# The slices' matmuls spread in four parts between the experts' layers

## The reference, cut to what matters

```
x = x + L0_gnn(layernorm(x), ...)        # first graph stage
x = x + L0_ffn(layernorm(x))             # top-2 experts
# second graph stage: attention over the edges
x_proj = (layernorm(x) @ W)
e_exp  = exp(alpha_src[row] + alpha_dst[col] - max over the edges of col)
out    = segment_sum(e_exp * x_proj[row], col) / segment_sum(e_exp, col)
x = x + out
# second expert stage: 8 dense experts of three layers on every node
feat = mean(layernorm(x)); w = softmax(feat @ Wr + br)
h = relu(bn(x_n @ W1 + b1)); h = relu(bn(h @ W2 + b2)); y = h @ Wo + bo
x = x + sum_e w_e * y_e
```

## Time and profile before

| | |
|---|---|
| runs (3), median | 5944.67 us |
| profiled execution, device time | 5958.87 us |
| its span | 5956.8 us |
| PE, share of the span | 4136.2 us, 69% |
| POOL, share of the span | 3178.3 us, 53% |
| DVE, ACT | 28%, 18% |
| granted TensorE clock, mean | 0.791 |

### The profile page before, as it was taken

How to read it: one execution, slowest core, us unless ns; L and a number is a source line. 1 busy time by engine, 2 the same in 40 slices (tenths; PEclk the granted TensorE clock), 3 DMA queues, 4 the chain that set the end, 5 groups by cost and what they waited for, 6 DMA issues and landing times. The chain is left out here.

```text
span 5956.8 us, 65813 instructions
## 1 busy us (share of the span) xinstructions
PE 4136.2 (69%) x20734; PEld 3330.2 (56%) x20734; DVE 1657.3 (28%) x5503; ACT 1082.2 (18%) x2144; POOL 3178.3 (53%) x3331
## 2 busy tenths in 40 slices
PE   1666666666666666666997267777777777777778
PEld 1665565656665656566886145554555455455546
DVE  5232322323222323233566011111121111112112
ACT  2010110101010101011564011121122112122212
POOL 5555555555555555553222665655555565556551
PEclk7777777777777777777998577877887787788779
DMA  5222222222222222221112433333333333333331
GB/s 170 73 83 84 83 83 85 80 86 80 85 81 83 82 83 83 83 82 54 59 48 68 133 94 99 96 93 98 96 98 91 98 97 94 96 96 100 92 97 42
DMA packets 223401, 522.56 MB, mean 88 GB/s; under 512 B 59660, under 2 KB 93918, under 8 KB 223332
## 3 DMA queue, kind: packets, MB, share of 16 engines
q0 software_dynamic: 155392, 430.52, 26.1%
q1 hardware_dynamic: 35768, 44.79, 2.4%
q10 hardware_dynamic: 32172, 46.39, 2.3%
HBM read 475.24 MB, written 46.24 MB: 88 GB/s over the span
## 5 line engine op out<-in xcount | busy, mean ns | idle before, releaser
L695 POOL DMA_INDIRECT ring<-xn,index x1588 | 1501.9, 946 | 1165.9 <-ACT index L708 693.1
L1697 POOL DMA_INDIRECT ring<-table,index x1616 | 1543.3, 955 | 1071.5 <-ACT index L1712 606.3
L814 PE MATMUL bank<-spare,ring 128*128 128x160 f32 x6448 | 1059.2, 328 | 265.4 <-issue 182.2
L814 PEld LDWEIGHTS bank<-spare,ring 128*128 128x128 f32 x6448 | 1022.9, 215 | 289.2 <-issue 217.7
L1892 PE MATMUL bank<-ring,acc 128*32 128x264 f32 x3232 | 577.6, 544 | 470.2 <-issue 415.0
L1766 ACT ACTIVATE ework<-bank,bn 128x256 f32<-128x256 f32 x800 | 406.5, 560 | 1506.2 <-remote 998.1
L824 PE MATMUL bank<-cells,wblk 128*128 128x128 f32 x1632 | 396.7, 365 | 399.2 <-issue 392.5
L1892 PEld LDWEIGHTS bank<-ring,acc 128*32 128x32 f32 x3232 | 187.5, 137 | 798.6 <-issue 774.0
L824 PEld LDWEIGHTS bank<-cells,wblk 128*128 128x128 f32 x1632 | 320.5, 262 | 467.5 <-issue 464.9
L1913 PE MATMUL bank<-acc,wa 128*128 (+1 forms) x1600 | 500.0, 463 | 90.9 <-ACT acc L1757 65.5
L824 PE MATMUL bank<-spare,wblk 128*128 128x128 f32 x1600 | 340.0, 355 | 286.9 <-issue 284.4
(11 more groups left out here) (272 smaller groups left out, 3019.9 us busy)
## 6 DMA issues: line engine op xcount, KB each, us to landing
ring<-table,index POOLq DMA_INDIRECT x1616
ring<-xn,index POOLq DMA_INDIRECT x1612
sums<-acc ACTq DMA_DIRECT2D x101, 132.0 KB
acc<-sums ACTq DMA_DIRECT2D x25, 264.0 KB
table<-frow SPq DMA_DIRECT2D x24, 264.0 KB, 3.0
nx<-in_x ACTq DMA_DIRECT2D x24, 256.0 KB
x<-nx ACTq DMA_DIRECT2D x24, 256.0 KB
fx<-x SPq DMA_DIRECT2D x24, 256.0 KB
```

What stands on the lines that cost most here:

```text
L695: pool.indirect_dma_start(ring[:, m * BT + t, :], None, k.xn_d, bass.IndirectOffsetOnAxis(ap=index[m][:, t:t + 1], axis=0)).then_inc(got[m ...
L814: ins = pe.matmul(win[q][:, h, :], ring[:, m * BT + q * QUAD + t, h * P:(h + 1) * P], onehot[:, (q * QUAD + t) % HELD, :], start=(t == 0), ...
L1697: pool.indirect_dma_start(ring[:, par * BT + t, :], None, k.table1_d, bass.IndirectOffsetOnAxis(ap=index[par][:, t:t + 1], axis=0)).then_i ...
```

## The change

PE no longer runs the 16 slice matmuls of batch b in one piece at the end of period b. It runs those of batch b-1 during period b in four parts of four matmuls: after layer 1 and layer 2 and layer 3 of sub-step 0, and after layer 1 of sub-step 1. The join of batch b-1 moves from sub-step 0 of period b to the end of that period. ACT's `keep_slices` and the staging of the next batch's offsets and index move from the period's start to behind layer 1's relu of sub-step 1; `move_window` and `keep_window` move to the period's end. DVE makes the next one-hots behind `gather_up` of sub-step 1 instead of that of sub-step 0.

```diff
@@ ACT, period
-                if window:
-                    keep_slices(b - 1)
-                if gathers and window:
-                    stage_near(b + 1, 1 - par)
-                    stage_index(b + 1, 1 - par)
...
                     for j2, e in experts(work_of, u, LAYER1):
                         relu(1, j2, e)
-                    if window and u == 0:
-                        move_window(b - 1, 1 - par)
-                        keep_window(b - 1, 1 - par)
+                    if window and u == 1:
+                        keep_slices(b - 1)
+                        if gathers:
+                            stage_near(b + 1, 1 - par)
+                            stage_index(b + 1, 1 - par)
...
                     for j2, e in experts(work_of, u, LAYER2):
                         relu(2, j2, e)
+                if window:
+                    move_window(b - 1, 1 - par)
+                    keep_window(b - 1, 1 - par)
@@ PE, slice_sums and period
-            def slice_sums(b, par, half, m, n):
-                pe.wait_ge(hots, b + 1)
...
-                for u in range(QUAD):
-                    for q in range(QUADS):
...
-                ins.then_inc(done, 1)
+            def slice_sums(b, par, half, u):
+                if u == 0:
+                    pe.wait_ge(hots, b + 1)
...
+                    for t in range(BT):
+                        wait_rows(pe, par, half, 0, 0, t)
+                for q in range(QUADS):
+                    t = q * QUAD + u
...
+                if u == QUAD - 1:
+                    ins.then_inc(done, 1)
...
+                last = (b - 1, 1 - par, half - 1 + par)
                 for u in range(2):
                     for j2, e in experts(work_of, u, LAYER1):
                         layer1(j2, e)
-                    if window and u == 0:
-                        join(b - 1, 1 - par)
+                    if window:
+                        slice_sums(*last, 3 * u)
                     for j2, e in experts(work_of, u, LAYER2):
                         layer2(j2, e)
+                    if window and u == 0:
+                        slice_sums(*last, 1)
                     for j2, e in experts(work_of, u, LAYER3):
                         layer3(j2, e)
+                    if window and u == 0:
+                        slice_sums(*last, 2)
+                    if window and u == 1:
+                        join(b - 1, 1 - par)
...
-                if gathers:
-                    slice_sums(b, par, half, m, n)
@@ DVE, period
-                if gathers:
-                    if not (isinstance(b, int) and b == 0):
-                        dve.wait_ge(windowed, b)
-                    one_hots(b + 1, 1 - par)
                 for j2, r in work_of:
                     if r == TURN + 2:
                         soft(j2)
                 for j2, e in experts(work_of, 1, GATHER):
                     gather_up(j2, e)
+                if gathers:
+                    if not (isinstance(b, int) and b == 0):
+                        dve.wait_ge(windowed, b)
+                    one_hots(b + 1, 1 - par)
                 for j2, r in work_of:
                     if r == TURN:
                         norm(j2)
```

More of the change, by code:

```diff
@@ L1881, in _ @@
             pe.wait_ge(p_load, 16 * 13)
-            def slice_sums(b, par, half, m, n):
-                pe.wait_ge(hots, b + 1)
-                if not (isinstance(b, int) and b == 0):
-                    pe.wait_ge(moved, b)
-                for t in range(BT):
-                    wait_rows(pe, par, half, m, n, t)
-                for u in range(QUAD):
-                    for q in range(QUADS):
-                        t = q * QUAD + u
-                        ins = pe.matmul(win[q * SLICE:(q + 1) * SLICE, :], onehot[:, par * BT + t, :],
-                                        ring[:, tile_at(par, m, t), :], start=(u == 0), stop=(u == QUAD - 1))
-                ins.then_inc(done, 1)
+            def slice_sums(b, par, half, u):
+                if u == 0:
+                    pe.wait_ge(hots, b + 1)
+                    if not (isinstance(b, int) and b == 0):
+                        pe.wait_ge(moved, b)
+                    for t in range(BT):
+                        wait_rows(pe, par, half, 0, 0, t)
+                for q in range(QUADS):
+                    t = q * QUAD + u
+                    ins = pe.matmul(win[q * SLICE:(q + 1) * SLICE, :], onehot[:, par * BT + t, :],
+                                    ring[:, tile_at(par, 0, t), :], start=(u == 0), stop=(u == QUAD - 1))
+                if u == QUAD - 1:
+                    ins.then_inc(done, 1)
             def join(b, par):
```

## The result

The changed kernel takes 6063.69 us (median of 4 runs, 6057.24 to 6070.47) against 5946.73 us for the kernel before (4 runs, 5944.37 to 5950.27): a ratio of 1.0198, 95% interval 1.0186 to 1.0210. It is 117 us slower; 148 us slower, 6093 us, was predicted. The profiled execution took 6070.47 us with a span of 6068.3.

The account below looks back on a forecast made before the run. PE was taken to be limited while a batch of gathers is under way. Transposition periods (24 x 5 = 120 us) and plain ones (28 us) summed to +148 us, giving 6093 us, own range 5985 to 6220.

Parts of the forecast that it names:

- the stall: PE's stretch of single MATMULs late in a batch's gathers, read as a limit beside gathers; 415.0 us idle before the slices.
- Term 1: PE's work ahead of done after the release, in periods without transposition: +0.4 us each, 28 us in all.
- upper bound: In plain periods, layer 1 and the last slice part follow the release at a low clock: 1.8 us more.
- lower bound: In plain periods, PE does all its work before the release: cycle 25.4 us, 0.6 us less.
- Term 2: Period with the transposition, where PE waits 8.4 us for one_hots and norm: +5 us, 24 times, 120 us.
- hand-made schedule: PE's pieces in the transposition's period timed from the first gather, G, to the next: 29.7 us, +3.7 us.
- the signal that I held to be late: The transposition's signal from PE to ACT, possibly 3 to 4 us late like the relu's: then +7 us.
- Term 3: Small costs: matmul shape switches, eight a period instead of two, hidden or 112 us; window's store, 0 to 3 us x 24.
- The stall goes: Rival: slices slow through themselves, so four early parts escape and the 415 us before them go; 5530 us, 7%.
- the clock stays down: Rival: PE's granted clock stays at 0.5 in free stretches, +4 us in every cycle; 6317 us, 8%.
- PE gets ahead: Rival: PE clears everything by the release in every period, each cycle 25.4 us; 5889 us, 10%.
- Only a rotation: Rival: terms 1 and 2 both near 0, no change; 5945 us, 5%.

Follow-up runs that it names:

- half_gathers: The kernel before with 8 of the 16 gathers of each merged-stage batch left out, slice matmuls reading the 8 gathered tiles twice: ratio 0.8337, 4967 us.
- tail_slices: The changed kernel with the fourth slice part right behind the third, and ACT's slice copy and casts ahead of layer 1's relu: ratio 1.0069 to the kernel before.
- norm_first: The changed kernel with DVE's norm put ahead of one_hots again: ratio 1.0168 to the kernel before.
- all_three: The changed kernel with norm ahead of one_hots, fourth slice part behind the third, index cast first, on chips without the stall: 0.9999, again 0.9996 to the kernel before.
- parted_done: The kernel before with done raised after each quarter of the slices, next gathers issued in quarters behind it, on chips without the stall: 0.9998, again 0.9998.
- norm_tail: The changed kernel with norm ahead of one_hots and the fourth slice part right behind the third: ratio 0.9982 to the kernel before.

## Why the prediction was right, and where it was not

The time, the sign and the mechanism came out: 6064 us measured for 6093, inside the own range of 5985 to 6220. The split of the sum did not: it was right as a sum because two terms were off in opposite directions, and that part of it is luck. Counted by the table, 44 us of the loss lie in the transposition's cycles, for which 120 were forecast, and 73 in the others, for which 28 were.

*What bounds.* The reading that the stall follows the gathers and not the slices held: half_gathers removed it (idle time before the slices 470.2 to 19.5 us), in the changed kernel it also sits on layer 1 and in tail_slices on layer 3. What the prediction could not know is that the program alone does not bring it about: three sets on other chips had none of it.

*Term 1, the tail of a plain period (+0.4 us taken, 28 us).* This is the step that failed most. Its upper bound had the tail as 14 MATMULs, six of them of layer 1, 3.4 us; measured in two of three plain periods: 13, 5.4 of layer 1, 3.4 to 3.5 us. I then chose a value near the lower bound, "after a period that kept PE at the full clock more is issued before the stall". It isn't: of the MATMULs between G and `done`, 69 to 74 came before the release in every kind of period before, and 70 or 71 in the three plain ones after. What differs is the kind of the MATMULs that are left, and the relu on ACT. With that relu counted in, the term is 77 us by tail_slices, 111 by the step from norm_first to norm_tail.

*Term 2, the transposition's period (+5 us taken, 120 us).* The wait was predicted at 8.4 us and is 8.40. But its cycle grew by 2.1 us, not 5, and taking the wait away gave 18 us alone and 52 with the tail mended. The hand-made schedule began with the join ending at G + 5; it ended at G + 2.8, since PE works on during ACT's copy and cast. The schedule also has a slip of 1 us: layer 2 at 1.7 us from 20 ends at 21.7, not 22.7, and the whole at 28.7, or +2.7 us, close to what was measured. And the signal that I held to be late by 3 to 4 us was not: layer 1 began 1.50 us after the transposition. That PE had not yet come to a stall there fits this, but was not tested. So this term had two sizes wrong: the +3.7 us of the schedule, 1 us too high by its own steps, and the 1.3 us more that were taken for the signal.

*Term 3, at nothing.* Nothing speaks against it, though no run tests it alone. The Trainium skill, "TensorEngine Tiling (Array Packing)", section "Key Properties", has it that a change of the tiling mode drains TensorE. Here a layer behind a slice part takes 1.99 us (layer 2 at 4745.52, where the clock was 1.00) and one behind another layer 1.89 (half_gathers' rows): the switch costs 0.1 us, where the prediction took 0.1 to 0.3, and the row that it took them from does not show the upper end, since the next work starts before it ends. On the chips without the stall PE is busy 30 to 43 us longer over the 87 cycles in all_three and all_three_again, with six switches a period, than in parted_done and parted_again, with two, again some 0.1 us a switch; the time is the same within 0.1%, since POOL bounds there.

*The rivals.* "The stall goes" and "the clock stays down" did not happen: the granted clock is 1.00 and 0.98 in the two free stretches read, and 0.79 over all 87 cycles against 0.80 before. "PE gets ahead" happened in single periods only. "Only a rotation" is what norm_tail shows: with both places mended the time is within 0.3% of before.

*What was to show it.* There are: cycles of 25.4 to 27.8 us for plain periods (in the mean of each kind; single ones took 24.3 to 29.7), PE idle 7 to 9 us before the transposition (the profile puts 8 of 24 down to DVE and 16 to "issue"), single steps on layer 1, and layer 1 ahead of `done` at a clock below full. Not there are cycles of 29 to 33 us once in four, which took 28.4, and single steps on layer 3, with 8.8 us in all.

## What to carry to other kernels

Where a batch of transfers is restarted by a signal from a slowed engine, its cost is the kind of work that stands last ahead of that signal: count what is left at the release, and put the cheapest pieces there. A helper's work that another engine waits for must not stand behind that engine's own last piece: DVE's 7 us of `norm` did, and PE's 8 us of waiting showed on both kinds of chip. And when two terms make up a sum, test each by undoing it alone and both together: here they gave 18 and 77 us alone, 128 together.

## What the runs showed of the hardware

The same program took 5942 to 5956 us on one chip and 4683 to 4685 us on others. The difference lies in stretches in which PE runs beside gathers: there PE works in single steps, mostly 0.7, 1.4 or 2.1 us apart, until 2.0 to 2.9 us behind the last gather's end, in the merged stage and in the first graph stage. In the merged stage the steps begin after a median of 60 to 65 MATMULs from the first gather, in each of the five kernels with 16 gathers that were counted, and by the release it is some 70. With 8 gathers a batch instead of 16 it does not come to that. The steps are not waits for code from memory: in the kernel before the DMA packets that bring instructions stop at 3662 us and come again at 5871 us, and the steps run on between.

The Trainium skill, "TensorE: Matmul & The Clock Gate", section "Architectural detail: the array is 16× 32×32, not 1× 128×128", gives TensorE an instruction queue of 64. That is near the 60 to 65 MATMULs before the single steps, but each of these comes with a weight load (20734 of each in the page), which such a queue might count too; no run here shows that the number has to do with it, or why only some chips do it. That they come with the gathers is shown, on this chip; their cause is open.
